# First stage of an attention and expert kernel written as one list of steps, with sends and sums moved to other engines

## The reference, cut to what matters

```python
def _L0_xattn_ref(q, k, v):          # q = layernorm(x), k = v = ctx, as (16, 128, 256)
    qh = q.reshape(b * h, d // h, m)     # h = 8 heads, d // h = 16
    kh = k.reshape(b * h, d // h, -1)
    vh = v.reshape(b * h, c // h, -1)
    qk = jnp.einsum('bdm,bdn->bmn', qh, kh) * scale
    sm = jax.nn.softmax(qk, axis=-1)
    ret = jnp.einsum('bmn,bcn->bcm', sm, vh)
...
x = x + _L0_xattn_ref(_layernorm(x, axis=-1), ctx_2048, ctx_2048)
x = x + _L0_ffn_ref(...)   # 16 experts; each takes its 128 highest rows of softmax(x @ router_w + router_b)
x = x + _L1_xattn_ref(...) # masked attention over the same ctx
x = x + _L1_ffn_ref(...)   # half of the rows of each batch through a gelu MLP
```

## Time and profile before

| | |
|---|---|
| median of three runs | 422.02 us (419.11 to 424.5) |
| the profiled execution | 422.43 us |
| its span, first to last instruction | 420.2 us |
| granted TensorE clock over the span | 0.841 |
| busy: PE, DVE, ACT, POOL | 279.6, 317.7, 167.6, 94.8 us |

### The profile page before, as it was taken

The page is one execution under the profiler, slowest core; times in us unless marked ns, Lnnn a source line. Parts: engine busy times, 40 slices in busy tenths (PEclk is TensorE's granted clock), DMA queues, the critical chain, the costliest instruction groups (busy, mean ns, idle before and its releaser), DMA issues.

```text
span 420.2 us, 7370 instructions
## 1 busy us (share of the span) xinstructions
PE 279.6 (67%) x1872; PEld 182.5 (43%) x1872; DVE 317.7 (76%) x989; ACT 167.6 (40%) x397; POOL 94.8 (23%) x222
## 2 busy tenths in 40 slices
PE   1134777777886877877778621001559999999996
PEld 0011333353442544444334310000438988888884
DVE  5847458899989889799986748888377888787631
ACT  4110543464654536464556500000111566445631
POOL 1101323352415224111111110000133322333200
PEclk9999975789698886899989965555555999999999
DMA  2789388959294581740000380000000000000001
GB/s 88 202 189 153 98 221 187 166 150 165 71 197 79 145 126 54 146 80 1 2 1 2 100 301 0 1 0 2 1 0 0 2 25 25 25 0 25 26 27 51
DMA packets 24379, 32.90 MB, mean 78 GB/s; under 512 B 4066, under 2 KB 22434, under 8 KB 22818
## 3 DMA queue, kind: packets, MB, share of 16 engines
q1 hardware_dynamic: 23842, 32.48, 33.5%
q10 hardware_dynamic: 512, 0.13, 0.2%
HBM read 24.02 MB, written 8.39 MB: 77 GB/s over the span
## 4 chain that ended last, share of the span: by engine, by line
DVE 35%; PE 33%; issue 12%; DMA 8%; ACT 4%; POOL 3%; SPq 2%; DVEq 1%; ACTq 1%; POOLq 0%
DVE row_max L531 7%; PE t_bank L1355 5%; PE pv_bank L1273 5%; PE pv_bank L1121 4%; DMA q_stack<-q_parts_dram 4%; DVE denom_inv L549 3%; PE score_bank L1094 3%; PE scoret_bank L1107 3%; PE t_bank L1150 2%; PE score_bank L1336 2%; DMA q_parts_dram<-q_parts 2%; ACT probs L895 2%; DMA q_stack<-neg_max 2%; PE score_bank L1303 2%; DVE junk L705 1%
## 5 line engine op out<-in xcount | busy, mean ns | idle before, releaser
L895 ACT ACTIVATE probs<-scoret_bank 128x512 f32<-128x512 f32 x128 | 73.1, 596 | 52.5 <-PE scoret_bank L1107 42.3
L531 DVE TENSOR_REDUCE row_max<-score_bank 128x2 f32<-128x512 f32 x112 | 74.4, 679 | 24.3 <-PE score_bank L1094 23.1
L1107 PE MATMUL scoret_bank<-q_stack,k_stack 98*128 98x256 bf16 (+1 forms) x256 | 54.6, 301 | 28.1 <-ACT probs L895 18.7
L1094 PE MATMUL score_bank<-k_stack,q_stack 96*128 96x256 bf16 (+1 forms) x240 | 53.6, 314 | 19.1 <-DMA q_stack<-q_parts_dram 11.0
L355 POOL TENSOR_SCALAR var_eps<-mv 128x1 f32<-128x1 f32 x48 | 9.2, 192 | 189.5 <-DVE mv L567 106.9
L1107 PEld LDWEIGHTS scoret_bank<-q_stack,k_stack 98*128 98x128 bf16 (+1 forms) x256 | 24.2, 104 | 46.6 <-ACT probs L895 20.5
L1121 PE MATMUL pv_bank<-probs,values_ones 128*32 128x256 f32 x512 | 42.0, 455 | 1.0 <-ACT probs L895 1.0
L1094 PEld LDWEIGHTS score_bank<-k_stack,q_stack 96*128 96x128 bf16 (+1 forms) x240 | 21.7, 105 | 47.8 <-issue 15.3
L1273 PE MATMUL pv_bank<-q_stack,k_stack 128*128 (+1 forms) x256 | 36.0, 285 | 0.4 <-ACT q_stack L1070 0.4
L1045 ACT COPY xnt<-score_bank 128x256 f32<-128x256 f32 x16 | 6.0, 373 | 74.6 <-PE score_bank L1294 74.6
L1273 PEld LDWEIGHTS pv_bank<-q_stack,k_stack 128*128 128x128 f32 x256 | 33.9, 202 | 1.3 <-issue 0.9
(11 more groups left out here) (182 smaller groups left out, 534.5 us busy)
## 6 DMA issues: line engine op xcount, KB each, us to landing
q_stack<-q_parts_dram SPq DMA_DIRECT2D x48, 128.0 KB, 6.9
k_parts_dram<-k_parts SPq DMA_DIRECT2D x24, 128.0 KB
q_parts_dram<-q_parts SPq DMA_DIRECT2D x24, 128.0 KB
k_stack<-k_parts_dram SPq DMA_DIRECT2D x8, 384.0 KB, 4.6
ctx_stage<-in_ctx_dram SPq DMA_DIRECT2D x8, 256.0 KB, 3.2
x_stage<-in_x_dram SPq DMA_DIRECT2D x8, 256.0 KB, 3.9
k_stack<-k_parts_dram SPq DMA_DIRECT2D x8, 256.0 KB, 5.3
xs<-in_x_dram SPq DMA_DIRECT2D x8, 256.0 KB, 7.3
```

The source lines that it names most:

```text
L531: dve.tensor_reduce(row_max[:, i, :, h], score_bank[bank_of][:, :].rearrange("p (m n) -> p m n", m=2), AX.X, ALU.max).then_inc(s["max_done ...
L895: act.activation(probs[:, j % PROBS, :], scoret_bank[j % 2][:, :], ACT.Exp).then_inc(s["exp_done"], 1)
L1094: ins = pe.matmul(to[:, m * D:(m + 1) * D], q_stack[0:QROWS, slot, h, b_in, m * P:(m + 1) * P], k_stack[0:QROWS, slot, h, b_in, :], start= ...
L1107: ins = pe.matmul(scoret_bank[j % 2][:, k * D:(k + 1) * D], k_stack[0:SROWS, slot, h, b_in, k * P:(k + 1) * P], q_stack[0:SROWS, slot, h, ...
```

## The change

1. On all engines the loops and unit functions of the first stage are replaced by one unrolled list over t = 0 to 127 and a tail, with tables for the step of each piece of work.
2. send_neg_max moves from ScalarE to SyncE's list, two steps behind neg_low.
3. The addition of x (x_new) moves from VectorE to GpSimd. The biases are split once by GpSimd into three bf16 rows and added by one more matmul in yw; y and logits lie side by side in y_ext and ScalarE copies both.
4. denom and numer lie side by side in gathered: ScalarE copies both low parts, VectorE gathers them in one operation over 512 columns.
5. Steps of the split: high_k(3) moves from step 8 to 10, mid_k from 10 to 13, high_q from 11 to 15, mid_q from 13 to 18. Unit 4: mid_q from 22 to 30. Unit 5: high_k from 29 to 34, mid_q from 36 to 42. Unit 6: high_k from 45 to 46, mid_q from 52 to 55. Unit 7: high_k from 61 to 62, mid_q from 68 to 71. Unit 2: mid_q from 4 to 6.
6. Tiles of the later stages (x_new3, z, attn and others) lie in k_stack's slots 2 and 3.

The diff, cut to its core:

```diff
-LEAD = NH
+LAST = STEPS * NU
...
+def ahead(t):
+    if t < NH:
+        return [STEPS + t]
+    if t < STEPS:
+        return [2 * t + NH, 2 * t + NH + 1]
+    return [t + STEPS + NH] if t + STEPS + NH < LAST else []
+MAX_T = {1: 0, 2: 9, 3: 16, 4: 21, **{b: NH * b - 14 for b in range(5, NB)}}
+NEG_HIGH = {b: MAX_T[b] + 3 for b in MAX_T} | {1: 1}
+NEG_LOW = {b: MAX_T[b] + 2 for b in MAX_T} | {1: 1, 2: 10}
+STAGE = {3: 10, 4: 22, 5: 34, 6: 46, 7: 62}
+MID_K = {2: 0, **{w: STAGE[w] + 3 for w in STAGE}}
+SCALE_Q = {2: 0, **{w: STAGE[w] + 2 for w in STAGE}}
+HIGH_Q = {2: 3, 3: 15, 4: 27, 5: 39, 6: 52, 7: 68}
+MID_Q = {w: HIGH_Q[w] + 3 for w in HIGH_Q}
+CTX_T = {2: 4, 3: 13, 4: 31, 5: 39, 6: 47, 7: 63}
+TAKE_VT = {2: 6, 3: 15, 4: 34, 5: 42, 6: 50, 7: 66}
+def due(table, t):
+    return [n for n in sorted(table) if table[n] == t]
+def before(table, t):
+    return min(table) + sum(1 for n in table if table[n] < t)
...
+            def send_neg_max(u, i):
+                sp.wait_ge(s["neg_done"], 2 * u + i + 1)
+                for part in range(2):
+                    sp.dma_start(q_stack[QROWS + part:QROWS + part + 1, u % SLOTS, :, i, :],
+                                 neg_max[:, i, part, :]).then_inc(neg_loaded[i], 16)
...
-            sp.wait_ge(neg_loaded[0], 32)
+            send_neg_max(0, 0)
...
-            def unit(u, more_stage, more_parts, reused):
-                wait_apart(sp, s["x_loaded"], 16 * (u + 1))
-                load_x(u + 1)
-                if more_parts:
-                    write_k_parts(u + 3)
-                    write_q_parts(u + 3)
-                    if more_stage:
-                        load_stage(u + 4)
-                    load_stacks(u + 3, reused)
...
+            for t in range(LAST):
+                for b in due(NEG_LOW, t - 2):
+                    send_neg_max(b // 2, b % 2)
+                for w in due(MID_K, t):
+                    write_k_parts(w)
+                for w in due(MID_Q, t):
+                    write_q_parts(w)
+                    if w + 1 < NU:
+                        load_stage(w + 1)
+                for w in due(MID_Q, t - 2):
+                    load_stacks(w, w >= SLOTS)
+                if t % STEPS == STEPS - 4 and t // STEPS + 1 < NU:
+                    wait_apart(sp, s["x_loaded"], 16 * (t // STEPS + 1))
+                    load_x(t // STEPS + 1)
...
+            def add_x1(b, u, i, first):
+                wait_apart(pool, s["div_step"], 4 * b + 4)
+                wait_apart(pool, s["x_loaded"], 16 * (u + 1))
+                if not first:
+                    wait_apart(pool, s["xn_ready"], b - 1)
+                    wait_apart(pool, s["kept"], b - 1)
+                pool.tensor_tensor(x_new[:, i, :], gathered[:, i, 1, :], xs[:, b, :], ALU.add).then_inc(s["x1_done"], 1)
...
+            def split_bias():
+                n = [0]
+
+                def step(ins):
+                    n[0] += 1
+                    ins.then_inc(s["bias_step"], 1)
+                    pool.wait_ge(s["bias_step"], n[0])
+
+                pool.wait_ge(s["w_small"], 16 * 9)
+                step(pool.tensor_copy(bias_terms[:, 0, :], bias_f[:, :]))
+                step(pool.tensor_tensor(bias_left[:, 0, :], bias_f[:, :], bias_terms[:, 0, :], ALU.subtract))
+                step(pool.tensor_copy(bias_terms[:, 1, :], bias_left[:, 0, :]))
+                step(pool.tensor_tensor(bias_left[:, 1, :], bias_left[:, 0, :], bias_terms[:, 1, :], ALU.subtract))
+                step(pool.tensor_copy(bias_terms[:, 2, :], bias_left[:, 1, :]))
+                for part in range(3):
+                    wait_apart(pool, s["ident_done"], 1)
+                    ins = pool.tensor_scalar(bias_kept[:, part, :], bias_terms[:, part, :], ident[0:3, part:part + 1], None, ALU.mult)
+                step(ins)
+                step(pool.tensor_tensor(bias_sum[:, :], bias_kept[:, 0, :], bias_kept[:, 1, :], ALU.add))
+                pool.tensor_tensor(bias_parts[:, :], bias_sum[:, :], bias_kept[:, 2, :], ALU.add).then_inc(s["bias_done"], 1)
...
+            for t in range(LAST + 3 * NH):
+                for b in range(NB):
+                    if t == NH * b + 17:
+                        root_rows(b, b % 2)
+                        keep_rows(x_new, b, b % 2)
+                for w in due(STAGE, t + 1):
+                    rest_k(w)
+                for w in due(STAGE, t - 1):
+                    root_q(w)
+                for w in due(MID_K, t + 1 if t else 0):
+                    low_k(w)
+                for w in due(HIGH_Q, t + 1):
+                    rest_q(w)
+                for w in due(MID_Q, t + 1):
+                    low_q(w)
+                for b in range(1, NB):
+                    if t == max(NH * b - 4, 2):
+                        fill_values(b, b // 2, b % 2, b < 2)
+                if t == NH + 1:
+                    split_bias()
+                for b in range(NB):
+                    if t == NH * b + 14:
+                        add_x1(b, b // 2, b % 2, b < 2)
...
-                odd_heads = pv_bank[i][:, D:2 * D]
                 dve.wait_ge(s["even_taken"], b + 1)
-                dve.scalar_tensor_tensor(denom[:, i, :], odd_heads, low[:, 0:1], sum_high[:, i, :],
+                if not (isinstance(b, int) and b < 2):
+                    dve.wait_ge(s["x1_done"], b - 1)
+                dve.scalar_tensor_tensor(gathered[:, i].rearrange("p k n -> p (k n)"), pv_bank[i][:, :], high[:, 0:1],
+                                         low_part[:, i].rearrange("p k n -> p (k n)"),
                                          ALU.mult, ALU.add).then_inc(s["div_step"], 1)
-                dve.scalar_tensor_tensor(numer[:, i, :], odd_heads, high[:, 0:1], num_low[:, i, :],
-                                         ALU.mult, ALU.add).then_inc(s["div_step"], 1)
...
+            def stage_a():
+                for t in range(LAST + 3 * NH):
+                    for n in (ahead(t) if t < LAST else []):
+                        maximum(n, n // NH, HEADS[n % NH], (n // NH) % 2, n % NH == 0, n % 2)
+                    for b in range(NB):
+                        i = b % 2
+                        if t == NH * b + 15:
+                            stats_x1(b, i)
+                        if t == NH * b + 17:
+                            scale_rows(b, i, b < 2)
+                        if t == NH * b + 10:
+                            gather_parts(b, i)
+                        if t == NH * b + 11:
+                            invert(b, i)
+                        if t == NH * b + 12:
+                            bring_over(b, i)
+                    for w in due(STAGE, t + 1):
+                        stats_q(w)
+                    for w in due(SCALE_Q, t):
+                        scale_q(w)
+                    for b in due(NEG_LOW, t):
+                        neg_low(b, b % 2)
...
+            def take_yw(b):
+                act.wait_ge(s["yw_ready"], b + 1)
+                act.copy(y_ext[:, b, :], t1_bank[:, 0:D + NE]).then_inc(s["yw_done"], 1)
...
-                act.mul(sum_high[:, i, :], pv_bank[i][:, 0:D], high[:, 0:1])
-                act.mul(num_low[:, i, :], pv_bank[i][:, 0:D], low[:, 0:1]).then_inc(s["even_taken"], 1)
+                    act.wait_ge(s["div_step"], 4 * (b - 2) + 1)
+                act.mul(low_part[:, i, 0, :], pv_bank[i][:, D:2 * D], low[:, 0:1])
...
+            for t in range(LAST + 3 * NH + 3):
+                if t < LAST:
+                    exponential(t // STEPS, t % STEPS, t < STEPS)
+                for b in range(NB):
+                    i = b % 2
+                    if t == NH * b + 26:
+                        take_yw(b)
+                    if t == NH * b + 10:
+                        take_even(b, i, b < 2)
+                    if t == NH * b + 23:
+                        take_xnt(b, i, b < 2)
+                for b in due(NEG_HIGH, t):
+                    neg_high(b, b // 2, b % 2)
+                for w in due(STAGE, t):
+                    high_k(w)
+                for w in due(MID_K, t):
+                    mid_k(w)
+                for w in due(HIGH_Q, t):
+                    high_q(w)
+                for w in due(TAKE_VT, t):
+                    take_vt(w)
+                for w in due(MID_Q, t):
+                    mid_q(w)
...
-                    ins = pe.matmul(t1_bank[:, 0:D + NE], xnt[:, i, k, :], wr_moving[:, k, :],
-                                    start=(k == 0), stop=(k == 1))
+                    pe.matmul(t1_bank[:, 0:D + NE], xnt[:, i, k, :], wr_moving[:, k, :],
+                              start=(k == 0), stop=False)
+                ins = pe.matmul(t1_bank[:, 0:D + NE], ones_bf[0:3, 0:P], bias_parts[:, :], start=False, stop=True)
...
+            for t in range(LAST + 3 * NH):
+                for n in (ahead(t) if t < LAST else []):
+                    if n % STEPS == 0:
+                        pe.wait_ge(s["stacks_loaded"], 144 * (n // STEPS + 1))
```

(20 more changed lines are left out.)

356 lines of the change are left out of this document (39 added, 317 removed).

## The result

| | before | after |
|---|---|---|
| median of the runs | 421.25 us (4 runs, 419.11 to 424.5) | 447.5 us (4 runs, 444.92 to 457.27) |
| ratio to before | 1 | 1.060, 95% interval 1.048 to 1.071 |
| span of the profiled execution | 420.2 us | 443.1 us |
| VectorE busy | 317.7 us | 298.2 us |
| forecast | | 420, range 406 to 433 |

One of the four runs of the changed kernel (457.27 us) fell into the chip's slower state; without it the median is 445.61, and the ratios in this document leave such runs out, so that where two kernels are compared the ratios decide over the medians.

The account below looks back on a forecast made before the run. VectorE, least idle from step 24 to 104, was taken as the bound. About 13 us won on pace and 11 lost on two late transfers made the span 420.2 - 1.8 us; the runs should give 420 us, range 406 to 433.

Parts of the forecast that it names:

- the late stack: At step 24, TensorE waits for unit 3's stack, 19.1 us behind its cast: T24 101.6, before 90.2, +11.4 us.
- the stacks come in time: Rival, 20%: cast to stack takes under 8.5 us, no stand at step 24, T24 91.0, total 410 us.
- The transfers get slower: Rival, 20%: units 3 to 6 crowd the DMA engines, cast to stack and stage 4 us more each, 432 us.
- the sum: Likeliest case, 45%, 414 to 427 us: step times added from T12 to T104 and the tail, giving 420 us.
- the second stand: At step 40, TensorE waits for unit 4's stack, a shorter stand near 127: T40 127.5, before 116.0.
- the stage waits: ScalarE and VectorE wait 3 to 4 us for x_stage near 113 and 134, the stage landing 8.3 us behind the cast.
- the pace: First-stage steps from 24 on, VectorE relieved by 0.98 us per batch: 1.40 us with splitting, 1.20 without.
- My upper bound: Step pace if TensorE or the GpSimd port takes the relief away: 1.50 and 1.30 us; rival, 15%, 426 us.
- what is behind the last step: Behind step 104: one send fewer on ScalarE, one bias matmul more, x_new by GpSimd in the last chain, -1.0 us.
- the sends: neg_max sends on SyncE's queue behind bulk loads: 0 us, at most 2 for batch 7; ScalarE gains only through waits.
- the cost of split_bias: Eleven GpSimd operations, once, 4.4 to 12.7 us, say 7, ending near 69, covered by the wait of step 12.
- GpSimd as a neighbour: x_new on GpSimd, 0.6 us per batch; through shared SBUF interfaces the added 9.6 us could at worst hold VectorE as long.

Follow-up runs that it names:

- e1: The changed kernel with TensorE's yw one step earlier (8b+22) and ScalarE's copy xnt two steps earlier (8b+21): 426.67 us, ratio to before 1.009.
- e9: e8 with ScalarE's take_yw at 8b+24 instead of 8b+26: 411.32 us, ratio to before 0.971.
- e8: e5 with SyncE's neg_max sends one step earlier in its list: 412.86 us, ratio to before 0.976.
- l1: e9 with the split and neg_max step tables put back to the changed kernel's late ones: 428.5 us.
- l2: e9 with the late split and neg_max tables, and split_bias at GpSimd's step 6 instead of 4: 425.76 us, ratio to before 1.012.
- e3: e1 with the split's step tables also set back to the steps of the kernel before: 417.54 us, ratio to before 0.989.
- e5: e3 with GpSimd's eleven split_bias operations moved from its step 9 to step 4: 413.25 us, ratio to before 0.980.

## Why the prediction was wrong, step by step

*Right: the late stack.* T12, T16 and T24 came within 0.7 us. Step 24 was late where and by as much as worked out, because the delay from cast to stack stayed what it had been three times: the cast starts at 82.76 (82.5 forecast) and

```profile
82.76 0.63 ACT L912 CAST q_parts<-q_rest 128x512 bf16<-128x512 f32 x1
...
91.33 0.58 PE L1035 MATMUL scoret_bank<-q_stack,k_stack 98*128 98x256 bf16 x2 [2.91 <-DMA q_stack<-neg_max]
...
101.48 0.61 PE L1022 MATMUL score_bank<-k_stack,q_stack 96*128 96x256 bf16 x2 [5.08 <-DMA q_stack<-q_parts_dram]
...
143.89 0.62 ACT L900 CAST k_parts<-ctx_stage 128x512 bf16<-128x512 f32 x1 [6.64 <-DMA x_stage<-in_x_dram]
```

TensorE starts on the stack 18.7 us behind the cast (19.1 forecast). The stand came in two pieces, since the scores of step 24 had first to wait for the send of batch 3, which SyncE issues at 87.61 behind the q parts and the stage. The rival "the stacks come in time" is refuted. "The transfers get slower", by 4 us each, is refuted too, though not wholly: by the landings in the trace it is 19.4, 18.7, 21.2, 19.2, 18.4 and 18.7 us from cast to stack for units 2 to 7, but from the cast of units 4, 5 and 6 to the next stage 10.2, 10.4 and 9.2 us, where the sum had 8.3. Stack 4 landed at 128.9, ahead of step 40 (130.9), so the second stand that the forecast named, near 127, did not come.

*Right in kind: the stage waits.* The last row is the one forecast at 134.5 to 138.8 us; ScalarE stood 6.6 us there, not 4.3, mainly because the stage landed 10.4 us behind the cast (133.46) instead of 8.3. The one forecast near 113 came at 118 with 1.5 us instead of 3 to 4, and ScalarE stood 4.4 us until 90.91 for the stage of unit 4, a wait that the forecast did not have; TensorE's stand at step 24 covers it.

*Wrong: the pace, "1.40 us with and 1.20 without splitting".* This is the step that failed. The changed kernel took 1.82 us per step from 24 to 72 (1.53 forecast, with the stage waits) and 1.36 from 72 to 103 (1.20 forecast). I took VectorE's busy time as the base and left 0.4 to 1.4 us of idle time in 16 steps, as if what VectorE waits for stayed the same; it was idle 8.1, 11.4, 5.9 and 5.0 us in the four stretches from step 24 to 88. My upper bound (1.50 and 1.30) assumed that at worst the relief is lost. That the list brings values, yw and the new bias matmul into one step of TensorE, so that VectorE must idle more than before, was no rival at all. With yw one step away (e1), T72, T88 and T103 are 173.9, 193.3 and 210.8, against 174.8, 194.0 and 212.0 in the sum: within 1.2 us. 20.8 of the 27.5 us are this. That the times meet so closely is in part luck: from 24 to 40 e1 took 27.0 us where the sum had 25.9, and from 56 to 72 20.6 where it had 22.4, since VectorE was busy 19.8 us there and not 22.0.

*Wrong: what is behind the last step, "-1.0".* From T103 to the start of the top-k it is 43.9 us, 40.4 before. In the changed kernel:

```profile
257.77 0.73 POOL L408 TENSOR_TENSOR x_new<-gathered,xs 128x256 f32<-128x256 f32 x1 [5.14 <-DVE gathered L603]
...
258.53 0.43 DVE L608 BATCH_NORM_STATS2 st<-x_new 128x6 f32<-128x256 f32 x1 [1.23 <-POOL x_new L408]
...
259.51 0.39 ACT L894 COPY y_ext<-t_bank 128x272 f32<-128x272 f32 x1 [2.23 <-PE t_bank L1080]
...
260.16 0.48 ACT L919 ACTIVATE low_part<-pv_bank,low 128x256 f32<-128x256 f32 x1
...
260.85 0.74 DVE L590 SCALAR_TENSOR_TENSOR gathered<-pv_bank,high,low_part 128x512 f32<-128x512 f32 x1
```

In the last batches nothing hides the hop to GpSimd and back: VectorE waits 1.23 us for a sum that took it 0.47. And ScalarE's list has take_yw of batch 13 ahead of low_part of batch 15, so the last division waits for a bias matmul. e1 still has 44.6 us from T103, where the forecast had 40.4 - 1.0. Its profiled span is 423.4 us against 418.4 in the sum: T103 is 1.2 earlier, this stretch 5.2 longer, and what follows the top-k start, which the change leaves alone but for places of tiles, 0.9 longer (168.0, 167.1 before; not explained). In the fastest version, e9, the stretch is 40.7 us. e9 differs from e8 (44.5) in take_yw alone, and l1 and l2, which have e9's take_yw and the late tables, have 40.7 too. So the place of take_yw most likely closes it; but these are single executions, and e3 and e5 have 41.9 with take_yw at its old step.

*Wrong in place and in weight: the sends.* They cost 2.9 us, where I had 0 to 2, and at batch 3, not at batch 7. What I missed is what they bring: ScalarE's issue time I counted as paying "only through waits that go", and the move is worth 15 us. On SyncE's queue a send took 3.7 us from issue to TensorE's start behind the stage loads (above), and 9.7 us behind the nine stack loads (e3, 85.92 to 95.67). The Trainium skill, DMA: Bandwidth & Descriptors, Queues, rings and completion order, says that SyncE and ScalarE each have a ring of their own on each of the 16 DMA engines, and that a DMA engine takes turns between the queues that it has work for. The two times agree with it for SyncE; no run here has the same send at the same time on ScalarE. The 15 us decide against ScalarE all the same.

*Right: the cost of split_bias.* Eleven operations were put at 7 us; they took 7.5. That they held nobody was right for the late tables and wrong for the early ones.

*About right: GpSimd as a neighbour.* x_new takes 0.72 us there (0.6 forecast) and VectorE's xn is no longer stretched (0.40 us in the row at 202.95, 1.18 in the earlier trace rows). Its place was taken by the product at the end of the division (L603): 1.03, 1.01 and 1.17 us at 73.32, 108.91 and 169.05, each beside a 128x512 subtraction of GpSimd (from 72.92, 108.49 and 168.78), and 0.43 elsewhere.

What the change is made of, by the runs: the sends on SyncE bring some 15 us and the sum moved off VectorE up to 4; the late split costs 14 to 17, yw beside the values 21 to 23. That makes a loss of some 16 to 25 us, against 26 measured. Parts that are measured in different surroundings don't add up exactly, and what the other parts of the change (the one gather, the bias matmul) bring or cost was not tried apart.

## What to carry to other kernels

When an order is written as a step list, write down for each engine what falls into the same step, and add up the longest run of work in which it does not feed its neighbour; here that run, against the two banks between them, set the pace, and not the busy time. The relief of the busiest engine brought nothing measurable while it was fed in bursts, and 3 to 4 us once it was fed evenly. In a forecast, carry as a rival the case in which the relieved engine waits more than before, since "the gain is lost" is no lower end.

## What the hardware showed that I had not expected

- The two kernels differ in TensorE's clock as well as in its waits. From step 24 to 103 the same matmuls (one yw more in e1) were busy for 94.0 us in the changed kernel and for 85.6 us in e1; the granted clock from step 40 to 88 was 0.78, 0.87 and 0.93, where e1 had 0.93, 1.00 and 1.00. yw's four matmuls took 1.08 us in the row at 190.52 (2.4 GHz) and 2.18 us in that at 198.77 (1.2 GHz). That the stands bring the low clock about is not shown: the fastest version had its lowest clock behind step 24, 0.73, from step 56 to 72, where TensorE stood still no longer than 1.2 us at a time.
- GpSimd's time for an operation hardly shrank with the number of partitions: 3x272 took 0.69 us where 128x256 took 0.72, and a multiplication by a column of 3x272 took 0.95 us each (2.85 for three).
- Two issues of 4 KB each on ScalarE took 1.29 us of its queue; with the wait for neg_low ahead of them ScalarE did no work for 2.15 us.
